# Reordering softmax sums in layer 0 of a two-layer transformer kernel

## The reference

```python
qkv = einsum('bnm,fm->bnf', x, Wqkv).reshape(b, n, 16, -1)
q, k, v = qkv[..., :8], qkv[..., 8:16], qkv[..., 16:]
scores = einsum('bnhd,bngd->bnhg', q, k) / 8.0
out = einsum('bnhg,bngd->bnhd', softmax(scores), v)
x = layernorm(x + out.reshape(b, n, -1) @ Wproj.T + bproj)
# gate: top 2 of 8 experts, softmax over the two, sum of the gated experts
x = layernorm(x + moe(x))
```

## Time and profile before

| | us |
|---|---|
| median of 3 runs | 2350.16 |
| lowest, highest | 2346.45, 2350.82 |
| the profiled execution, its own time | 2345.11 |
| its span | 2343.3 |

### The profile page before, as it was taken

The page is one execution under the profiler, slowest core; times in us unless marked ns, Lnnn a source line. Parts: engine busy times, 40 slices in busy tenths (PEclk is TensorE's granted clock), DMA queues, the critical chain, the costliest instruction groups (busy, mean ns, idle before and its releaser), DMA issues. The chain is left out here.

```text
span 2343.3 us, 63240 instructions
## 1 busy us (share of the span) xinstructions
PE 2127.8 (91%) x16512; PEld 1590.6 (68%) x16513; DVE 1819.2 (78%) x6003; ACT 1571.4 (67%) x4002; POOL 1079.6 (46%) x2292
## 2 busy tenths in 40 slices
PE   5999999998799999999999999999999948999950
PEld 3777767776577766766776676667667638998850
DVE  6888888884388888888888888888888855666658
ACT  2555555555388777878777787787778735666655
POOL 4766667665123443344344434443443343555432
PEclk7999999999799999999999999999999978999985
DMA  1000000000100000000000000002000011112125
GB/s 33 24 20 27 20 27 20 27 20 12 51 2 7 11 15 11 11 11 15 9 13 11 15 6 14 13 13 84 17 16 11 11 32 51 56 55 55 54 71 173
DMA packets 80485, 66.90 MB, mean 29 GB/s; under 512 B 10220, under 2 KB 75384, under 8 KB 79754
## 3 DMA queue, kind: packets, MB, share of 16 engines
q1 hardware_dynamic: 71804, 47.27, 6.9%
q0 software_dynamic: 8448, 16.86, 2.2%
HBM read 33.61 MB, written 22.62 MB: 24 GB/s over the span
## 5 line engine op out<-in xcount | busy, mean ns | idle before, releaser
L1327 DVE SCALAR_TENSOR_TENSOR restT<-ps_t,leadT 128x512 f16<-128x512 f32 (+1 forms) x768 | 458.6, 597 | 130.7 <-ACT leadT L1261 96.6
L1261 ACT ACTIVATE leadT<-ps_t 128x512 f16<-128x512 f32 (+1 forms) x768 | 402.5, 524 | 144.8 <-PE ps_t L1127 143.8
L1110 PE MATMUL ps_s<-xT_all,qm 128*128 128x512 f32 (+1 forms) x1024 | 489.8, 560 | 0.8 <-ACT qm L1242 0.8
L1127 PEld LDWEIGHTS ps_t<-ident,p 128*128 128x128 f32 x2560 | 317.2, 141 | 228.6 <-issue 169.3
L1127 PE MATMUL ps_t<-ident,p 128*128 128x128 f32 x2560 | 412.7, 276 | 6.1 <-DVE restT L1327 4.5
L1252 ACT ACTIVATE p<-ps_s,neg_max 128x512 f32<-128x512 f32 (+1 forms) x512 | 325.4, 636 | 73.5 <-DVE neg_max L1317 62.9
L1317 DVE CUSTOM_DVE_ANT_0 ps_s<-ps_s,mask 128x512 f32<-128x512 f32 (+1 forms) x512 | 319.7, 624 | 44.6 <-PE ps_s L1110 41.0
L982 POOL CAST v_parts<-v_all 128x36 bf16<-128x36 f32 x256 | 57.2, 223 | 614.4 <-PE ps_o L1141 614.4
L1110 PEld LDWEIGHTS ps_low<-xT_all,qm 128*128 128x128 f32 x1024 | 195.1, 191 | 135.8 <-issue 122.5
L1101 PE MATMUL ps_qm<-xT_all,m_head 128*128 128x512 f32 x512 | 266.5, 602 | 2.2 <-POOL m_head L970 0.8
L261 POOL TENSOR_TENSOR pv_prod<-probs,kv 128x2048 f32<-128x2048 f32 x64 | 259.6, 4074 | 0.1
(11 more groups left out here) (225 smaller groups left out, 4310.2 us busy)
## 6 DMA issues: line engine op xcount, KB each, us to landing
row_in<-rows_dram SPq DMA_DIRECT2D x136, 64.5 KB
y<-results SPq DMA_DIRECT2D x32, 256.0 KB, 3.3
xT<-in_xT SPq DMA_DIRECT2D x32, 128.0 KB, 2.1
xres<-in_xT SPq DMA_DIRECT2D x32, 128.0 KB, 2.1
xT_all<-x2T SPq DMA_DIRECT2D x32, 128.0 KB, 2.0
x_all<-rows SPq DMA_DIRECT2D x16, 256.0 KB, 2.6
out_x<-x SPq DMA_DIRECT2D x16, 256.0 KB, 2.2
xT_all<-in_wide SPq DMA_DIRECT2D x1, 2760.0 KB
```

Source lines behind the costliest of these rows:

```text
L1110: mm = pe.matmul(ps_s[n], qm[j][:, n * P:(n + 1) * P], xT_all[:, bass.ds(b * S, (n + 1) * P)], start=True, stop=True)
L1127: mm = pe.transpose(ps_t[g][:, at + n * P:at + (n + 1) * P], probs[i][:, n * P:(n + 1) * P], ident[:, :])
L1261: act.activation(leadT[j][g][:, :], ps_t[g][:, 0:width[g]], ACT.Copy, scale=RAISE)\
L1327: dve.scalar_tensor_tensor(out=restT[j][g][:, :], in0=ps_t[g][:, 0:width[g]], scalar=RAISE, in1=leadT[j][g][:, :], op0=ALU.mult, op1=ALU.s ...
```

## The change

Three orders in layer 0 are changed. No instruction is added or removed.

```diff
 # GpSimd
                 def step(u, j, part):
+                    if part[3]:
+                        inverse1(*before(u, j, 2))
                     if part[2]:
                         normalise(*before(u, j, 1))
-                    if part[3]:
-                        inverse1(*before(u, j, 2))
                     if part[2]:
                         pv_products(*before(u, j, 1), 0)
                         pv_products(*before(u, j, 1), 1)
 # ScalarE
                     if part[2]:
                         copy_oT(*before(u, j, 1))
+                    if part[1]:
+                        exponentials(u, j)
                     if part[4]:
                         copy_x2T(*before(u, j, 3))
-                    if part[1]:
-                        exponentials(u, j)
 # VectorE
                     if part[1]:
                         qk_products(u, j, 0)
+                    if part[2]:
+                        exp_sums(*before(u, j, 1))
+                        exp_recips(*before(u, j, 1))
+                    if part[1]:
                         qk_products(u, j, 1)
                     if part[4]:
                         moments_2(*before(u, j, 3))
...
                         qk_sums(u, j)
                         find_max(u, j)
                         shift_scores(u, j)
-                        exp_sums(u, j)
-                        exp_recips(u, j)
```

## The result

The changed kernel takes 2403.95 us, median of 4 runs from 2403.62 to 2404.89; the kernel before takes 2350.21 beside it. The ratio is 1.0231, 95% interval 1.0214 to 1.0248. It is slower by 53.7 us; 53.0 were forecast.

What follows compares the result with a forecast made beforehand. TensorE's fixed order was taken to bound the 17.00 us step, then a loop of 18.72 us: 2.1 + 48.2 + 2.9 + 0.7 us, sum 53.9, less 0.9 for the clock dip, 53.0 on 2350.16, 2403.2 us; range 2390 to 2416.

Steps and rivals of the forecast that it cites:

- TensorE bounds the step, GpSimd is 1.46 us from it: Layer 0, kernel before: TensorE's fixed order sets the 17.00 us step; GpSimd's second value product is done 1.46 us early.
- the path over `inverse1` and `norm1`: GpSimd, new order: `inverse1`, ahead of `normalise`, needs only `moments_1` and finishes while VectorE is at the query-key product.
- The loop of 18.72 us: Layer 0, projection through statistics, one query-key product, reciprocals, `normalise`, value products and `sum_heads` to next projection: 18.72 against 17.00 us.
- The steps at full clock: Layer 0, steps 3 to 30: 28 times 1.72 us more, 48.2 us.
- step 31: Layer 0, no new query-key-value product: 15.83 us before, held at 18.72 by the loop, 2.9 us more.
- step 32: Layer 0, no query-key products: 16.48 against 15.74 us, 0.7 us more.
- The first steps: Layer 0: step 1 takes 2.1 us more; step 2, already 19.31 us with TensorE at half clock, nothing more.
- The fall near 484 us: Layer 0: a clock dip costing 2.9 us before; new slack could hide 1.7, of which half, 0.9, was taken off.
- Waits after: Layer 0: VectorE waits some 2.9 us a step for the projection; TensorE waits twice for value products, some 1.7 together.
- VectorE as the bound: Rival, layer 0: VectorE sets the pace, so its 1.19 us wait is pure gain: 35 us, 2315 us; chance 4%.
- The delay is not hidden: Denies a rival: GpSimd's two value products in 6.5 us instead of 8.13, leaving 2350 us; chance 3%.
- The falling clock: Rival, TensorE in layer 0: two more 0.8 us pauses bring clock dips, 34 to 81 us more, 2437 to 2484; chance 7%.

Runs made afterwards that it cites:

- 2.24 taken out by order: The changed kernel with the sums and reciprocals ahead of both query-key products, directly behind `moments_1`: 2349.71 us, ratio 0.9978.
- 1.94 by size: The changed kernel with GpSimd's value products cut to 12 of 16 key heads: 2356.2 us, ratio 1.0011.
- 1.13 put in: The changed kernel with one further GpSimd product into a scratch tile ahead of `normalise`: 2450.47 us, ratio 1.0410.
- `probs * probs`: The kernel before with one more GpSimd instruction of 1.06 us between `inverse1` and the value products: 2317.31 against 2322.14 us, ratio 0.998.
- the kernel in which TensorE stood idle for 3.45 us: The kernel before with only VectorE's sums and reciprocals moved between the query-key products, GpSimd and ScalarE in old order: 2556.14 us, ratio 1.0856.

## Why the prediction was right, step by step

- *TensorE bounds the step, GpSimd is 1.46 us from it.* VectorE given 0.94 us and GpSimd's value products put back by 1.06 us changed nothing, so neither bounds. That TensorE does follows from its timeline (busy 16.16 of 17.03 us, and a pause for `copy_v`); no run makes its list shorter, so it is argued and not shown by itself. Incomplete in one point: the path over `inverse1` and `norm1` has only some 0.6 us to spare. The prediction checked that this path would not be late in the new order and did not ask how near it was in the old one.
- *The loop of 18.72 us.* The 28 steps from 3 to 30 took 529.7 us in the changed kernel. Without 5.7 us for two falls of the clock that is 18.71 a step. 2.24 taken out by order or 1.94 by size make it shorter than TensorE's 17.0, and the loss is gone; 1.13 put in shows whole.
- *The steps at full clock.* 48.9 us more in steps 3 to 30, 48.2 forecast; 2.7 in step 31 (18.49 us) and 0.8 in step 32 (16.55), 2.9 and 0.7 forecast.
- *The first steps.* Off: step 1 ended 2.7 us later and not 2.1 (L344 at 41.40 against 38.68), and step 2 took 19.90 and not 19.31. TensorE's clock is at half for part of them, and its rise does not come at the same place in each run: the same L344 stands at 39.68 in the kernel with ScalarE's edit alone, which has the order of before there: 1.0 us later than in the kernel before. These terms were short by 1.2 us in all.
- *The clock.* The fall near 484 us cost the kernel before 2.9 us. The changed kernel had two, one of 4.5 us at 119 and one of 1.2 at 498 (steps of 23.05 and 19.83 us, where steps of their kind take 18.59). The second is as forecast: 2.9 less the 1.7 the new slack hides. The first is larger than the prediction allowed for one, with 13.7 us at half clock and not 6.8. It need not belong to the new order: in the same step, step 6, the clock also fell with ScalarE's edit alone (19.88 us), with the sums ahead of both products (19.84) and with `probs * probs` (23.06), and did not in the kernel before.
- *The sum.* 48.9 (steps 3 to 30) + 2.7 and 0.6 (steps 1 and 2) + 2.7 and 0.8 (steps 31 and 32) + 5.7 for the two falls − 2.9 for the one of before is 58.5, and the last projection does end 58.5 us later (626.07 against 567.58). The medians are 53.7 apart, since the profiled execution of the kernel before was 5 us faster than its median. So the agreement with 53.0 to within 1 us is partly luck: half a fall of the clock was taken off in the forecast, and the run had more of them, on top of a fast run of before.
- *Waits after.* VectorE's wait was 3.6 us a step, not 2.9: of the 1.45 us of other pauses that were kept in the sum, 0.65 are left in a step (18.60 less 14.47 busy less 3.48), since VectorE now comes late to some of what it had waited for. TensorE's two waits, 0.54 and 0.58 us in the step shown and 1.3 a step on average, were not 1.7 together. The delay is nearly all there all the same: in the step shown the two `sum_heads` start 1.35 and 1.60 us after the instruction ahead of them, where it had been 0.65 and 0.86, so 0.70 and 0.74 later; before, the product ahead had overlapped their start, and that part is not listed as a wait.
- *Rivals.* VectorE as the bound fell with ScalarE's edit alone and with the sums ahead of both products. The delay is not hidden: no value product got shorter. The falling clock did not decide this kernel, but its price was real: VectorE's edit alone pays it in every step. The Trainium skill's advice to optimize first the engine with the highest occupancy, TensorE being judged by its weight loads, names VectorE here (Perfetto Trace Analysis, Identifying the Most-Contended Engine). It did not hold in this kernel: 0.94 us a step given to VectorE brought nothing.

## What to carry to other kernels

Where engines run fixed orders side by side, follow the semaphores once around and add up the loop: moving a wait off a busy engine is worth nothing if the moved work then stands in a longer loop, and here one product of 2.24 us in the wrong place made a path with 1.46 us to spare the bound. Two paths out of one queue have each their own slack: an instruction ahead of GpSimd's small four cost 0.5 us a step at full clock and falls of the clock besides, one as long behind them nothing. Ask of each edit what it brings alone: two of these three made no loss, and one of them, GpSimd's, kept the third from costing four times as much.

## What the runs showed of the hardware

TensorE's granted clock, at 2.4 GHz in nearly all of the kernel before, fell to 1.2 GHz in every step of the kernel in which TensorE stood idle for 3.45 us, and stayed there for 6.8 us in most steps and 10.2 in the others (311.0 to 321.2 above), at 3.3 us a step. It also fell without such a pause: in nine of 28 steps with one more GpSimd instruction, in the step shown right behind a pause of 0.62 us for `copy_v` (358.0 to 361.0 above), where the steps had two further pauses of 0.3 us shortly after that one. The sum of the pauses does not order these kernels. From 160 to 480 us the pauses that TensorE's timeline lists add up to 18.0 us in the kernel before, where the clock never fell, to 18.3 with one more GpSimd instruction, where six falls began, and to 37.8 in the changed kernel, where it never fell. Where the pauses stand may matter; what decides between a fall and none was not settled. A fall cost from 0.9 us (in the changed kernel with one more instruction) to 6.1 (step 6 with `probs * probs`, 23.06 us for 16.97), depending on how long it lasted and how much of it lay in slack.
